# Row maxima of the tokenwise attention taken over pairs of PSUM banks, with score rows eight tiles ahead

## What is computed

```
weight = einsum('bct,bcs->bts', q * scale, k * scale)      # 64 blocks of 512 x 512
h = einsum('bts,bcs->bct', softmax(weight, -1), v)         # the tokenwise attention
h = h + attn(layernorm(h), Wq, Wk, Wv, Wo)                 # 16 heads, rope, window 128
h = h + ffn(layernorm(h), w1, w2, w3)                      # ternary weights: gate, product, down
```

## Time and profile before

| | |
|---|---|
| runs | 1132.97, 1137.09, 1140.35 us |
| profiled execution | 1134.29 us, span 1132.3 us, mean granted TensorE clock 0.961 |
| busy: PE, DVE, ACT, POOL | 89%, 62%, 39%, 47% of the span |
| tokenwise stage | 0 to 362.3 us of the span |
| later stages | 362.3 to 1132 us |
| row maxima, L421 | x256, 163.5 us busy |
| exponentials, L378 | x256, 138.8 us busy |
| score rows, L560, and columns, L575 | x256 each, 122.1 and 111.0 us busy |

### The profile page before, as it was taken

One profiled execution on the slowest core, in us unless ns is written; L12 is line 12 of the kernel. 1 busy time (PEld: TensorE's weight loads), 2 busy tenths in 40 slices (PEclk: granted clock), 3 DMA queues, 4 the chain that ended last, 5 costly groups with the idle time before them and its releaser, 6 DMA issues.

```text
span 1132.3 us, 20343 instructions
## 1 busy us (share of the span) xinstructions
PE 1010.5 (89%) x7776; PEld 558.8 (49%) x7776; DVE 704.4 (62%) x1273; ACT 439.8 (39%) x761; POOL 536.9 (47%) x434
## 2 busy tenths in 40 slices
PE   4888896888862679999999999999999999999996
PEld 2433332333310336466575664765756646657554
DVE  6667675878754437565576575655765757557642
ACT  1778783768752213132141231321412313214221
POOL 2576673577683615345155253451552534515510
PEclk9999998989986879999999999999999999999998
DMA  8979874655422111100101011101010111010100
GB/s 250 279 270 296 268 232 120 178 179 149 141 87 66 28 19 30 38 28 19 37 19 37 28 28 37 28 19 37 19 37 28 28 37 28 19 37 19 28 10 19
DMA packets 70580, 92.12 MB, mean 81 GB/s; under 512 B 39312, under 2 KB 40080, under 8 KB 70544
## 3 DMA queue, kind: packets, MB, share of 16 engines
q1 hardware_dynamic: 70544, 91.66, 27.4%
HBM read 49.43 MB, written 8.39 MB: 51 GB/s over the span
## 4 chain that ended last, share of the span: by engine, by line
PE 56%; issue 4%; DVE 3%; POOL 2%; ACT 1%; DMA 1%; SPq 0%; POOLq 0%; DVEq 0%
PE ffn_sum L1106 7%; PE ffn_sum L1107 7%; PE proj L1169 5%; PE proj L1171 5%; PE proj L1170 5%; PE proj L1064 3%; PE proj L1066 3%; PE proj L1065 3%; PE transposed L1058 3%; DVE ctx_lo L964 2%; PE ffn_sum L1066 2%; PE ffn_sum L1064 2%; PE ffn_sum L1065 2%; PE ffn_sum L1155 2%; PE transposed L1142 1%
## 5 line engine op out<-in xcount | busy, mean ns | idle before, releaser
L795 POOL TENSOR_TENSOR roped<-rope_cos,rope_sin 128x512 f32<-128x512 f32 x80 | 101.6, 1270 | 249.9 <-DVE rope_sin L933 249.9
L421 DVE TENSOR_REDUCE row_max<-score_rows 128x1 f32<-128x512 f32 x256 | 163.5, 677 | 57.4 <-PE score_rows L560 57.0
L1106 PE MATMUL ffn_sum<-x_hi,ffn_w 128*128 128x128 f16 x1408 | 167.5, 220 | 7.7 <-DMA x_lo<-x_lo_rows 7.7
L378 ACT ACTIVATE exps<-score_cols 128x512 f32<-128x512 f32 x256 | 138.8, 599 | 76.2 <-PE score_cols L575 75.5
L1107 PE MATMUL ffn_sum<-x_lo,ffn_w 128*128 128x128 f16 x1408 | 167.3, 220 | 0.0
L1106 PEld LDWEIGHTS ffn_sum<-x_hi,ffn_w 128*128 128x128 f16 x1408 | 138.4, 99 | 13.0 <-DMA x_lo<-x_lo_rows 8.2
L560 PE MATMUL score_rows<-k_parts,q_parts 96*128 96x512 f32 x256 | 122.1, 492 | 22.0 <-DMA k_parts<-qk_split 13.9
L1107 PEld LDWEIGHTS ffn_sum<-x_lo,ffn_w 128*128 128x128 f16 x1408 | 138.8, 99 | 2.3
L575 PE MATMUL score_cols<-q_parts,k_parts 98*128 98x512 f32 x256 | 111.0, 441 | 26.8 <-DMA q_parts<-max_lo 14.4
L560 PEld LDWEIGHTS score_rows<-k_parts,q_parts 96*128 96x128 f32 x256 | 53.0, 208 | 112.1 <-DVE row_max L421 55.1
L314 POOL TENSOR_TENSOR exp_sums<-exps 128x512 f32<-128x512 f32 x64 | 80.7, 1291 | 52.4 <-PE score_rows L560 31.0
(11 more groups left out here) (124 smaller groups left out, 1977.9 us busy)
## 6 DMA issues: line engine op xcount, KB each, us to landing
q_parts<-qk_split SPq DMA_DIRECT2D x45, 256.0 KB, 4.0
k_parts<-qk_split SPq DMA_DIRECT2D x45, 256.0 KB, 4.5
attn_slots<-in_w_attn SPq DMA_DIRECT2D x20, 512.0 KB, 6.6
ffn_w<-in_w_ffn SPq DMA_DIRECT2D x12, 704.0 KB, 8.9
qk_split<-in_qk SPq DMA_DIRECT2D x15, 512.0 KB, 4.2
raw_ffn<-in_w_ffn SPq DMA_DIRECT2D x9, 704.0 KB, 4.6
v_t<-in_v_t SPq DMA_DIRECT2D x16, 256.0 KB, 5.2
h_rows<-tok_out_sum SPq DMA_DIRECT2D x16, 256.0 KB, 4.3
```

Source lines behind the costliest of these rows:

```text
L378: nc.scalar.activation(E[:, n % NE, :], ST[n % 3][:, :], ACT.Exp, scale=TOK_SCALE).then_inc(exp_done, 1)
L421: nc.vector.reduce_max(row_max[:, g % 2, k:k + 1], S[n % NS][:, :], AX.X).then_inc(s_free, 1)
L795: nc.gpsimd.tensor_tensor(rope[:, c, :], ra[c % 2][:, :], rb[c % 2][:, :], ALU.add).then_inc(added, 1)
L1106: nc.tensor.matmul(dst, w, x2h[:, k, :], start=(k == 0), stop=False)
```

## The change

The four banks of score rows become two tensors of two banks each; score columns have two banks in place of three. TensorE fills both halves of a pair with two matmuls and signals once, after the second. VectorE takes both maxima in one instruction with two results. The transposed maxima and a total take a whole pair of the ring each. Rows run 8 tiles ahead (`MAX_AT` = 10), `total` moves to u = 5, `weigh` from the steps 8, 10, 13, 17 to 7, 10, 14, 17. VectorE turns, inverts and applies the sums behind the pairs that end with 11, 13 and 15, and `scales` comes behind the pair 14, 15 of group 9.

```diff
-LOOK, TAKE = 7, 1
+LOOK, TAKE = 8, 1
-DEN_AT = STEPS + 3
+DEN_AT = STEPS + 5
+TURN_AT = LOOK + DEN_AT - STEPS - 2
+    entries = [entry for entry in entries if entry[0] != "row" or entry[2] % 2 == 0]
-        NB, NV, NE, NS, NO = 3, 2, 3 * GB, 3, 2
+        NB, NV, NE, NS, NC, NO = 3, 2, 3 * GB, 2, 2, 2
-        S = [pb(f"score_rows{n}") for n in range(NS)]
-        ST = [pb(f"score_cols{n}") for n in range(3)]
+        S = [ctx.enter_context(nc.psum_tensor(f"score_rows{n}", [P, 2, T], FP32)) for n in range(NS)]
+        ST = [pb(f"score_cols{n}") for n in range(NC)]
-        SCALES_AT = 14
-        OUT_AT = {8: 0, 10: 1, 13: 2, 17: 3}
+        OUT_AT = {7: 0, 10: 1, 14: 2, 17: 3}
...
-                nc.vector.reduce_max(row_max[:, g % 2, k:k + 1], S[n % NS][:, :], AX.X).then_inc(s_free, 1)
+                nc.vector.reduce_max(row_max[:, g % 2, k:k + 2], S[n % NS][:, :, :], AX.X).then_inc(s_free, 1)
...
-                for k in range(STEPS):
-                    maximum(r, k)
+                for k in range(1, STEPS, 2):
+                    maxima(r, k - 1)
...
-                    if k == LOOK + 1 and r >= 2:
+                    if k == TURN_AT and r >= 2:
                         turn_sums(r - 2)
-                    if k == LOOK + 2 and r >= 2:
+                    if k == TURN_AT + 2 and r >= 2:
                         invert(r - 2)
-                    if k == LOOK + 3 and r >= 2:
+                    if k == TURN_AT + 4 and r >= 2:
                         finish(r - 2)
-                    if k == SCALES_AT and r == MEASURED + 1:
+                    if k == STEPS - 1 and r == MEASURED + 1:
                         scales()
...
-                bank = enter_ring(ring["row", g, k])
-                nc.tensor.matmul(bank[:, :], QP[g % NB][0:3 * CH, b, t * P:(t + 1) * P], KP[g % NB][0:3 * CH, b, :],
-                                 start=True, stop=True).then_inc(s_full, 1)
+                n = ring["row", g, k - k % 2]
+                bank = enter_ring(n) if k % 2 == 0 else S[n % NS]
+                product = nc.tensor.matmul(bank[:, k % 2, :], QP[g % NB][0:3 * CH, b, t * P:(t + 1) * P],
+                                           KP[g % NB][0:3 * CH, b, :], start=True, stop=True)
+                if k % 2 == 1:
+                    product.then_inc(s_full, 1)
...
-                pe.wait_ge(s_free, ring["row", g, STEPS - 1] + 1)
+                pe.wait_ge(s_free, ring["row", g, STEPS - 2] + 1)
...
-                if n >= 3:
-                    pe.wait_ge(exp_done, n - 2)
+                if n >= NC:
+                    pe.wait_ge(exp_done, n - NC + 1)
```

More of the change, by code:

```diff
@@ L377, in exps @@
                     act.wait_ge(stacked[1], copies(1))
-                nc.scalar.activation(E[:, n % NE, :], ST[n % 3][:, :], ACT.Exp, scale=TOK_SCALE).then_inc(exp_done, 1)
+                nc.scalar.activation(E[:, n % NE, :], ST[n % NC][:, :], ACT.Exp, scale=TOK_SCALE).then_inc(exp_done, 1)
             def bound_attn(c):
@@ L417, in _, with maxima @@
         def _(dve):
-            def maximum(g, k):
+            def maxima(g, k):
                 n = ring["row", g, k]
                 dve.wait_ge(s_full, n + 1)
-                nc.vector.reduce_max(row_max[:, g % 2, k:k + 1], S[n % NS][:, :], AX.X).then_inc(s_free, 1)
+                nc.vector.reduce_max(row_max[:, g % 2, k:k + 2], S[n % NS][:, :, :], AX.X).then_inc(s_free, 1)
             def take_transposed(g):
@@ L435, in turn_sums @@
                 dve.wait_ge(s_full, n + 1)
-                nc.vector.transpose(den_t[:, :, :].rearrange("p k c -> p (k c)"), S[n % NS][:, :]).then_inc(s_free, 1)
+                nc.vector.transpose(den_t[:, :, :].rearrange("p k c -> p (k c)"), S[n % NS][:, 0, :]).then_inc(s_free, 1)
             def invert(g):
@@ L558, in rows @@
                     pe.wait_ge(stacked[g % 2], copies(g))
-                bank = enter_ring(ring["row", g, k])
-                nc.tensor.matmul(bank[:, :], QP[g % NB][0:3 * CH, b, t * P:(t + 1) * P], KP[g % NB][0:3 * CH, b, :],
-                                 start=True, stop=True).then_inc(s_full, 1)
+                n = ring["row", g, k - k % 2]
[4 more added lines that the diff above has]
+                    product.then_inc(s_full, 1)
             def transpose_maxima(g):
-                pe.wait_ge(s_free, ring["row", g, STEPS - 1] + 1)
+                pe.wait_ge(s_free, ring["row", g, STEPS - 2] + 1)
                 bank = enter_ring(ring["max", g])
-                nc.tensor.transpose(bank[0:STEPS, 0:P], row_max[:, g % 2, :], ident[:, :]).then_inc(s_full, 1)
+                nc.tensor.transpose(bank[0:STEPS, 0, 0:P], row_max[:, g % 2, :], ident[:, :]).then_inc(s_full, 1)
             def cols(g, u):
@@ L572, in cols @@
                     pe.wait_ge(max_in, 2 * DMA * (g + 1))
[L573 to L575 removed]
+                if n >= NC:
+                    pe.wait_ge(exp_done, n - NC + 1)
+                nc.tensor.matmul(ST[n % NC][:, :], KP[g % NB][0:3 * CH + 2, b, i * P:(i + 1) * P],
                                  QP[g % NB][0:3 * CH + 2, b, :], start=True, stop=True).then_inc(st_done, 1)
@@ L593, in total @@
                 for b in range(GB):
-                    nc.tensor.matmul(bank[b * CH:(b + 1) * CH, :], ones[:, :], SUM[:, b, :], start=True, stop=False)
+                    nc.tensor.matmul(bank[b * CH:(b + 1) * CH, 0, :], ones[:, :], SUM[:, b, :], start=True, stop=False)
                 for i in range(DEPTH[g] + 1, NT):
                     for b in range(GB):
-                        last = nc.tensor.matmul(bank[b * CH:(b + 1) * CH, :], ones[:, :],
+                        last = nc.tensor.matmul(bank[b * CH:(b + 1) * CH, 0, :], ones[:, :],
                                                 E[:, (STEPS * g + GB * i + b) % NE, :], start=False, stop=(i == NT - 1))
```

5 lines of the change are left out of this document (2 added, 3 removed).

## The result

The median goes from 1136.87 us (4 runs, 1132.97 to 1140.35) to 1151.93 us (4 runs, 1150.86 to 1154.85), a ratio of 1.0134 with a 95% interval of 1.0105 to 1.0163: 15 us more. The forecast was 1145, with a range of 1130 to 1156 and 1141 to 1149 for its main case: the measured time lies inside the range, outside the main case, and beyond the one per cent to which the forecast gave 0.32. The profiled execution of after took 1150.86 us (span 1148.8, mean granted clock 0.955), 16.5 us more span than that of before.

A forecast was written before the change was run, and what follows sets the result against it. The prediction took TensorE, the q and k load chain and the weight-splitting loop to bound successive parts of the stage; its terms summed to +7.9 us, giving a median of 1145 us, range 1130 to 1156.

The forecast's parts named there:

- main case: The prediction's own account of the whole kernel: 1141 to 1149 us, chance 0.50.
- rival 2: New TensorE waits make the clock fall three to five times more, +8 to +14 us on top, 1153 to 1159; chance 0.20.
- The pair at 1.17: VectorE's paired reduction of row maxima, in no earlier trace: taken as 1.17 us, allowed from 0.65 to 1.35.
- The stall of 1.05 before row 2: In each group TensorE waits for the first pair's reduction before the third score row: 1.05 us, a new stall.
- (c): Weight splitting from group 11: a 19.73 us loop through ScalarE and GpSimd sets the period; 1.7 us longer, +5.1 over three.
- Groups 9 and 10, +2.2: Two TensorE-bound groups: shorter period -0.8, later `total` +0.5, fewer column banks +1.4, so +1.1 us each.
- The scales and the period before, +0.1: One TensorE-bound period before the scales, -0.8 us, and a longer wait for the last maxima at the scales, +0.9.
- (b): Until about 163 us the chain of q and k loads, raise and stacking, 16.8 us a turn, sets the pace: 0 change.
- Tail +0.5: From 313 to 362 us, `total` of group 14 comes two steps later and delays only sums: +0.5 us.
- kind (a): Periods where TensorE is the bound with short waits: 15.9 us against 16.75, so -0.8 each.
- Rival 1: TensorE is the bound everywhere: 13 periods win 0.8 us, the scales cost 0.9, so -9.5, 1128 us; chance 0.17.
- Rival 3: Two column banks bind ScalarE in groups 1 to 8 too: +4 to +5 us, 1149; chance 0.13.

The follow-up runs named there:

- pair_two_reduces: The changed kernel with each pair reduced by two instructions, the second of which frees it: 1150.26 us, ratio 1.0122.
- pair_col_first: The changed kernel with the score column of step 12 issued ahead of that step's score rows: 1139.99 us, ratio 1.0028.
- order_only: The kernel before with the change's new order alone, three row and three column banks, single maxima: 1128.04 us, ratio 0.9929.
- order_rows4_cols2: The kernel before with the new order, four single row banks and two column banks, no pairs: 1137.81 us, ratio 1.0011.
- light_weigh: The kernel before with the second to fourth products with v of groups 1 to 6 cut to 128 of 512 columns: 1137.29 us, ratio 1.0014.
- pair_warm: The changed kernel with six extra matmuls into an unused bank ahead of column 0 of group 0: 1146.15 us, ratio 1.0086.
- pair_weigh11: The changed kernel with the second `weigh` at step 11 in place of 10: 1141.99 us, ratio 1.004.
- rows4_cols2: The kernel before with four single row banks and two column banks, no pairs, old order: 1140.64 us, ratio 1.0025.
- order_warm: order_only with the column of step 12 first and six extra matmuls before column 0 of group 0: 1129.41 us, ratio 0.9929.
- pair_total3: The changed kernel with `total` back at step 3 and VectorE's work on sums two maxima earlier: 1144.27 us, ratio 1.0061.

## Why the prediction was right, and where its sum was not
The direction came true, through the stall at row 2 and the later periods, and the time lies in the range. It lies outside the main case (1141 to 1149): the sum of 7.9 was 8.6 short in the profiled execution, since 9.0 us arose in the two places to which it gave nothing. The range held because its upper end was drawn for rival 2, falls of the clock inside the periods of the stage; what filled it came from the start and from the later stages. So the sum was right in the middle, and that the total stayed inside the range is luck. (The 0.32 for slower is also a little under what its own parts add up to, about 0.20, 0.06 and 0.10.)

- **The pair at 1.17**: right, 1.18, and harmless by itself (pair_two_reduces).
- **The stall of 1.05 before row 2**: right in place and size, 0.98. What I priced was its length. Its weight lies in what stands behind it in TensorE's order: the column of step 12. I counted it in the loop of (c) as a piece of the 1.7, and pair_col_first shows that piece to be 0.96: period 21.00 with it, 20.04 without, though `below` overlaps GpSimd's operation again there (2.49 us), which takes 0.36 off the gain.
- **Three periods of (c), +5.1**: +4.5 measured, and not as worked out. Two of them are 1.3 us longer than the earlier trace rows, where 1.7 was forecast; the third, 21.66, has a fall, as the second of before had. The walk also left out what the order takes off: with three single banks each the period is 18.97 (order_only), with four and two 20.16 at a clock of 0.92 and 19.78 at 1.00 (order_rows4_cols2), with pairs 21.00. So it reads -0.8 for the order, +0.8 to +1.2 for the lost column bank, and the rest for the pairs.
- **Groups 9 and 10, +2.2**: +1.7. Here two errors met: before's own stretch had a fall (22.53 us at 0.85), and both periods of after have one too, smaller, at 0.92.
- **The scales and the period before, +0.1**: +1.4. The period came 0.6 us longer (172.15 to 189.49 is 17.34, and the earlier trace rows has 16.75) where the walk gave 15.9. The walk let each column go when TensorE reached it; in the trace TensorE waits for exponentials 18.8 us between 30 and 330 us, 9.3 before. Two banks for columns are what the walk left out. That the wait for the maxima's store would go came true.
- **(b) holds until 163 us, so 0**: right as a lower bound, and the zero is wrong. From 77.90 on the turns are as long as before, and the queue waited 24.3 us for the stacking (24.5 in the earlier trace rows). The five turns take 90.03 us in before, 90.71 in the change, 89.68 in order_only and 91.12 in light_weigh: nothing made them shorter by more than 0.4. But the chain starts behind the exponentials of the first group, and there two banks for columns, mostly by the later rise of the clock (pair_warm brings back 2.7 to 3.5), made it 5.0 us late.

  Nor does the chain close on itself, as I wrote: the high part stands behind an exponential in ScalarE's order, and score tiles do enter through it. The same five turns take 92.0 to 94.9 us in pair_weigh11, rows4_cols2, pair_col_first, order_warm and order_rows4_cols2. In pair_col_first the cast goes straight behind an exponential that waited for its column, 1.9 us after its data had landed, where before's waited for the DMA (152.34):
```profile
159.21 0.60 ACT L379 ACTIVATE exps<-score_cols 128x512 f32<-128x512 f32 x1 [0.84 <-PE score_cols L579]
159.71 1.04 ACT L363 CAST qk_split<-qk_split 128x1024 fp32r<-128x1024 f32 x1
```

- **Later stages stay, so 0**: their work stayed; the clock in them didn't (+3.4).
- **Tail +0.5**: 0.0.
- **The order**: my walk gave it to the change as 0.5 + 0.7 us a period, mostly eaten. Alone it is worth 8 to 9 us (order_only), which I didn't see, since I gave (c) no gain. A steady period of kind (a) wins 1.6 us there (15.13), and one of kind (c) 0.76, the 0.75 that GpSimd's operation no longer loses to `below`. The place of `total` isn't what does that: pair_total3, with `total` back at step 3, has 2.13 too, and so has the change. No run moves `below` alone.
- **Rival 1** (TensorE bound everywhere): refuted until 163 us by order_only, and by light_weigh as far as it goes, and behind that by (c). **Rival 3** (two column banks): true at 1.0056, though at the start and in (c), and little in groups 1 to 8 (the five turns take 91.28 us for 90.03). **Rival 2** (clock): three of five periods at 0.92 (21.42, 21.46 and 21.66 us), and 3.4 us in the later stages. pair_warm has the same periods at 0.92, 1.00 and 1.00, with 21.40, 21.00 and 19.97 us, so that a fall costs up to 0.5 us where the loop (c) holds and 1.7 in the last period:
```profile
300.89:320.86 19.97, 16.80 (x89) 6.34 (x88) 15.72 (x16) 15.17 (x22) 11.59 (x8) 1.00 0.28 101
```
  My 2.8 us a fall was too high for either. Before has falls of its own in three of these periods (0.85, 0.91, 0.92), so that the falls in the stage add nothing that can be shown.

By kernels the 15 us read: order and four single row banks with two for columns +1 together (the order -9, the lost column bank +6, the fourth row bank -3, which is within the noise, and some 7 that the order loses with two column banks); pairs +14, of which 12 go when column 12 is issued ahead of the wait. Those 12 hold 4.3 us of the later stages and what the change's three falls cost, so they are what the edit did to the time, not the price of the wait alone; free of falls that is 1 us a period.

The Trainium skill, page "TensorE: Matmul & The Clock Gate", section "A second HAM failure mode: psum-queue depth-cycling", says that short idle times while banks are cycled can make the clock swing. The traces agree in kind: 0.92 in three periods of the change, 1.00 in all five of pair_col_first. Their price here was 0.5 us in one period and 1.7 in another.

## What to carry to other kernels
Where an engine takes its work in one order, price a new wait by what stands behind it, not by its length: a wait of 1 us a group came with 12 us of 1152, which went when one unrelated matmul was issued ahead of it, though the wait itself stayed at 0.75 us. Fewer, larger buffers (two pairs for four banks) have the ring length of their number: a small entry that takes a whole one halves the ring for a moment. And test the parts of such a change apart: here the new order alone was worth 8 us and was hidden under the banks that came with it.

## What the runs showed of the hardware
- One reduction over two adjacent banks, 128x1024, takes 1.18 us back to back, two over single banks 0.61 each: the edge between the banks costs nothing that shows.
- At the start score tiles run at 0.63 us each until 37.5 us in before and 43.3 in after, and the granted clock of these stretches reads 1.00; quick ones take 0.39. The trace has no record of the clock there, and the durations tell what the row can't.
- With three banks for score columns tiles get quick at 36.9 to 38.7 us, with two at 41.9 to 48.1.
- With 13 us of matmul work taken away, in one trace, the granted clock fell from 0.98 to 0.89: work removed from a TensorE that isn't the bound is partly paid back in slower matmuls.
- GpSimd's 128x1024 product with fp16 output takes 2.13 us, and 2.49 to 2.88 where it overlaps VectorE's TENSOR_SCALAR 128x1408 from fp32 to fp16 (25 of 25 from 190 to 320 us). The one that starts second is the one that gets longer. Beside reductions or SCALAR_TENSOR_TENSOR it stays at 2.13. In order_only none overlaps (mean 2.14 of 17, for 2.39 of 15 before).
- The same instructions of the later stages take up to 5 us more or less by when the clock rises in them.
